# A selective scan of four batches and its preparation, put into one stage

## The reference

```python
A = -jnp.exp(A_log)
xp = jnp.einsum('bld,rd->blr', x, x_proj_w)
dt_in, B, C = xp[..., :16], xp[..., 16:32], xp[..., 32:]
dt = jax.nn.softplus(jnp.einsum('blr,dr->bld', dt_in, dt_proj_w) + dt_proj_b)
dA = jnp.exp(dt[..., None] * A)
dBx = dt[..., None] * B[:, :, None, :] * x[..., None]
# over the 512 tokens of a batch:
#   h = dA_t * h + dBx_t ;  y_t = sum over n of h[:, n] * C_t[n]
y = ys + D * x
```

## Time and profile before

| | us |
|---|---|
| runs | 2249.59, 2257.28, 2246.22 (median 2249.59) |
| profiled execution | 2264.58 |
| its span | 2262.8 |
| mean granted clock of TensorE | 0.9 |

### The profile page before, as it was taken

The page is one execution under the profiler, slowest core; times in us unless marked ns, Lnnn a source line. Parts: engine busy times, 40 slices in busy tenths (PEclk is TensorE's granted clock), DMA queues, the critical chain, the costliest instruction groups (busy, mean ns, idle before and its releaser), DMA issues. The chain is left out here.

```text
span 2262.8 us, 27810 instructions
## 1 busy us (share of the span) xinstructions
PE 1836.9 (81%) x8232; PEld 1117.8 (49%) x8232; DVE 1625.3 (72%) x2905; ACT 808.6 (36%) x1301; POOL 734.1 (32%) x582
## 2 busy tenths in 40 slices
PE   6287878787759899945994888888864999999998
PEld 2022222222436788833881333333452777787786
DVE  4699999999644466666205888888468777667668
ACT  5243434333211344421222777777523111111112
POOL 2676767665250466665002000000021333113100
PEclk7599999999878689866996999999985999999999
DMA  8111111110130688854544333333000000000002
GB/s 302 23 42 38 37 38 35 39 33 15 35 135 14 205 278 285 287 180 130 195 194 126 87 95 91 91 94 87 4 30 28 29 29 29 1 29 29 1 1 75
DMA packets 102032, 197.64 MB, mean 87 GB/s; under 512 B 17257, under 2 KB 34025, under 8 KB 101019
## 3 DMA queue, kind: packets, MB, share of 16 engines
q1 hardware_dynamic: 96795, 179.46, 24.7%
q0 software_dynamic: 5120, 16.78, 2.3%
HBM read 130.72 MB, written 63.05 MB: 86 GB/s over the span
## 5 line engine op out<-in xcount | busy, mean ns | idle before, releaser
L1527 DVE TENSOR_REDUCE att_top<-att_first 128x1 f32<-128x512 f32 x512 | 332.4, 686 | 104.0 <-PE att_first L1407 96.2
L421 PE MATMUL scan_y<-scan_hc,all_ident 128*128 128x512 f32 x512 | 294.8, 663 | 102.2 <-DVE scan_hc L381 102.2
L355 POOL TENSOR_TENSOR scan_dbx<-ssm_U,scan_bbc 128x512 f32<-128x512 f32 x256 | 316.0, 1267 | 135.6 <-DVE scan_h L390 101.9
L390 DVE TENSOR_TENSOR_SCAN scan_h<-scan_da,scan_dbx 128x512 f32<-128x512 f32 x256 | 310.4, 1213 | 23.6 <-POOL scan_dbx L355 20.0
L1489 ACT ACTIVATE att_prob<-att_second 128x1024 f32<-128x1024 f32 x256 | 248.0, 1022 | 88.5 <-PE att_second L1427 83.1
L366 ACT ACTIVATE scan_da<-ssm_DT,ssm_A 128x512 f32 x256 | 176.7, 691 | 271.5 <-DVE scan_h L390 271.4
L421 PEld LDWEIGHTS scan_y<-scan_hc,all_ident 128*128 128x128 f32 x512 | 79.0, 194 | 314.7 <-DVE scan_hc L381 314.0
L1673 POOL TENSOR_TENSOR pairs_raw<-pairs_raw,pairs_scales 128x512 f32<-128x512 f32 x42 | 42.4, 1044 | 526.6 <-DMA pairs_raw<-in_w 526.6
L1803 ACT ACTIVATE ffn_silu<-ffn_pg 128x256 f32<-128x256 f32 x112 | 43.1, 385 | 414.7 <-PE ffn_pg L130 414.7
L1407 PE MATMUL att_first<-att_ks,att_qs 48*128 48x512 f32 x512 | 133.9, 512 | 63.3 <-DVE att_top L1527 48.5
L128 PE MATMUL ffn_pg<-pairs_wh,last_XH 128*128 128x512 f32 x448 | 180.3, 402 | 1.7 <-PEq L431 1.7
(11 more groups left out here) (272 smaller groups left out, 3917.4 us busy)
## 6 DMA issues: line engine op xcount, KB each, us to landing
mlps_raw<-in_w SPq DMA_DIRECT2D x26, 769.0 KB, 6.0
exp_raw<-in_w SPq DMA_DIRECT2D x24, 769.0 KB, 6.0
scan_bbc<-brow_dram SPq DMA_DIRECT2D x64, 256.0 KB, 3.1
sorted_x<-pre_zero SPq DMA_DIRECT2D x4, 3072.0 KB, 15.4
exp_x<-sorted_x SPq DMA_DIRECT2D x48, 256.0 KB, 3.9
sorted_y<-exp_y SPq DMA_DIRECT2D x48, 256.0 KB, 3.8
att_qs<-qk_dram SPq DMA_DIRECT2D x192, 64.0 KB, 2.2
att_ks<-qk_dram SPq DMA_DIRECT2D x192, 64.0 KB, 2.2
```

The source lines that it names most:

```text
L355: nc.gpsimd.tensor_tensor(dbx[:, i % (2 * KC), :], g.U[:, c, bass.ts(b, NB)], bbc[:, n % RING, :], ALU.mult).then_inc(dbx_ready, 1)
L390: nc.vector.tensor_tensor_scan(h[:, i % HRING, :], da[:, i % 2, :], dbx[:, i % (2 * KC), :], 0.0, ALU.mult, ALU.add).then_inc(h_ready, 1)
L421: mm = pe.matmul(y[:, c, :], g.ident[:], hc[:, i % 2, :], start=(m == 0), stop=(m == STATE - 1))
L1527: nc.vector.tensor_reduce(top[w % 2][:, qt, item:item + 1], p_first[first_place(m) % FIRSTS][:], AX.X, ALU.max).then_inc(max_done, 1)
```

## The change

The two stages become one, `ssm`. Only batch 0 is prepared ahead of the first scan, by short instructions of one block each; batch b + 1 is prepared while batch b is scanned, and the magnitudes and positive parts of batch b + 2 are read then as well.

- Lists are unrolled over 64 states (4 batches x 16). Buffers of dt, u, mag, pos hold two batches.
- One ACT copy takes all 80 rows. B's and C's rows are both stored to HBM.
- C is split by VectorE into two float32r parts (`split_c`), at partitions 64 and 96, and spread by one product over both (`spread`), into a `cbc` of one bank instead of two. The free bank is `aux`, for rows, z and dt's sums.
- POOL's four products of a state become one of 128x2048, B's row repeated by a stride of zero (`inputs`).
- For c = 3, POOL weighs instead of VectorE (`weigh_last`), with C's row loaded by a broadcast DMA into `cbs`, where `pooled(n)` holds: all but states 5 and 6 of batches 0 to 2.
- For batches 1 to 3 ACT makes the positive part (Relu), 1 + e, its negative rest (Identity) and the mask (Sign); POOL multiplies the logarithm by the mask; PE adds the four parts of dt by products with the identity (`sum_dt`); ACT copies it out.
- The zeros for `sorted_x` go out as 48 DMAs of 256 KB, one per state from n = 4. x of batch 0 is loaded first.
- The sums of batch b - 1 stand between the scans of states 0 and 2 of batch b.

The core of the diff:

```diff
+        def pooled(n):
+            return n // STATE == BATCH - 1 or n % STATE not in (5, 6)
...
+            store_rows(0)
+            for n in range(STEPS):
+                b, m = n // STATE, n % STATE
+                if m == 0:
+                    sp.wait_ge(stored[b % 2], 32 * (b // 2 + 1))
+                if n >= RING:
+                    sp.wait_ge(dbx_ready, n - RING + 1)
+                sp.dma_start(bbc[:, n % RING, :], g.brow_dram[m, b].partition_broadcast(P)).then_inc(b_in[n % RING], 16)
+                if pooled(n):
+                    if by_pool(n) >= RING:
+                        sp.wait_ge(hp_ready, by_pool(n) - RING + 1)
+                    sp.dma_start(cbs[:, by_pool(n) % RING, :], g.crow_dram[m, b].partition_broadcast(P)
+                                 ).then_inc(c_in[by_pool(n) % RING], 16)
...
+            def inputs(n):
+                pool.wait_ge(b_in[n % RING], 16 * (n // RING + 1))
+                if n % STATE == 0:
+                    pool.wait_ge(u_ready, made(n // STATE, LAST))
+                if n >= 2:
+                    pool.wait_ge(h_ready, KC * (n - 1))
+                nc.gpsimd.tensor_tensor(dbx[:, n % 2], u[:, n // STATE % 2],
+                                        bbc[:, n % RING, :].unsqueeze(1).to_broadcast([P, KC, NB]),
+                                        ALU.mult).then_inc(dbx_ready, 1)
...
+                if n >= 2 and pooled(n - 2):
+                    weigh_last(n - 2)
+                if b + 1 < BATCH:
+                    if m in (7, 8):
+                        masked_ln(b + 1, 2 * (m - 7))
+                        masked_ln(b + 1, 2 * (m - 7) + 1)
+                    if m in (11, 12, 13, 15):
+                        scaled_x(b + 1, (11, 12, 13, 15).index(m))
...
+                nc.scalar.activation(da[:, i % 2, :], dt[:, b % 2, c, :], ACT.Exp,
+                                     scale=minus_a[:, c, n % STATE:n % STATE + 1]).then_inc(da_ready, 1)
+                if b + 2 < BATCH:
+                    if j == 8:
+                        copy_rows(b + 2)
+                    if j in (13, 17, 21, 25):
+                        magnitude(b + 2, (j - 13) // 4)
+                    if j in (14, 18, 22, 26):
+                        positive(b + 2, (j - 14) // 4)
                 if b + 1 < BATCH:
+                    if j < 4:
+                        exponential(b + 1, j)
+                    if 4 <= j < 8:
+                        one(b + 1, j - 4)
+                    if 9 <= j < 13:
+                        negative_rest(b + 1, j - 9)
+                    if j == 15:
+                        logarithm(b + 1)
+                    if j in (16, 19, 20, 23):
+                        mask(b + 1, (16, 19, 20, 23).index(j))
+                    if j in (35, 40, 46, 51):
+                        copy_dt(b + 1, (35, 40, 46, 51).index(j))
...
+            split_c(0)
+            for c in range(KC):
+                positive0(c)
+            for c in range(KC):
+                rest0(c)
+                low0(c)
+            for c in range(KC):
+                part0(c)
+            for c in range(KC):
+                masked_ln0(c)
+                sum0(c)
+                scaled_x0(c)
+            split_c(1)
...
+                    if c:
+                        weigh(n, c - 1)
+                    elif n and not pooled(n - 1):
+                        weigh(n - 1, LAST)
...
+                for k, part in enumerate((mag[:, b % 2], u[:, b % 2], pos[:, b % 2], ln)):
+                    mm = pe.matmul(aux[:], g.ident[:], part[:, c, :], start=(k == 0), stop=(k == 3))
...
+                for c in range(LAST):
+                    if c == LAST - 1 and pooled(n) and n + 1 < STEPS:
+                        spread(n + 1)
+                    gather(n, c)
+                    if n >= 2 and c == 0 and pooled(n - 2):
+                        gather(n - 2, LAST)
+                    if b + 2 < BATCH:
                         if m == 0:
+                            project_rows(b + 2, c)
+                        if m == 1 and c == 0:
+                            project_rows(b + 2, LAST)
+                        if 2 <= m < 2 + KC and c == 1:
+                            project_z(b + 2, m - 2)
+                    if b + 1 < BATCH and (m, c) in ((7, 1), (8, 2), (10, 0), (11, 1)):
+                        sum_dt(b + 1, ((7, 1), (8, 2), (10, 0), (11, 1)).index((m, c)))
```

More of the change, by code:

```diff
@@ L238, in _ @@
[L238 to L252 removed]
+                nc.scalar.activation(rows[:, b % 2, :], aux[0:ROWS, :], ACT.Copy).then_inc(rows_copied, 1)
@@ new lines, in z_of, with magnitude @@
+            def z_of(b, c):
+                return y[:, c, :] if b < 2 else aux[:]
+            def magnitude(b, c):
+                act.wait_ge(z_ready, KC * b + c + 1)
+                if b == 2:
+                    act.wait_ge(low0_ready, c + 1)
+                    act.wait_ge(ln_ready, 1)
+                if b > 2:
+                    act.wait_ge(dt_summed, made(b - 2, c))
+                nc.scalar.activation(mag[:, b % 2, c, :], z_of(b, c), ACT.Abs, bias=dtb[:, c:c + 1]).then_inc(mag_ready, 1)
@@ new lines, in project_z @@
+            def project_z(b, c):
+                pe.wait_ge(rows_copied, b + 1)
+                if b == 1:
+                    pe.wait_ge(mag_ready, c + 1)
+                    pe.wait_ge(pos0_ready, c + 1)
+                if b >= 2:
+                    pe.wait_ge(c_lo_ready, b + 1)
+                    pe.wait_ge(pos_ready, KC * (b - 1) + c)
+                out = y[:, c, :] if b < 2 else aux[:]
+                pe.matmul(out, wdt[:, c * P:(c + 1) * P], rows[0:RANK, b % 2, :], start=True, stop=True).then_inc(z_ready, 1)
@@ new lines, in spread, with gather @@
+            def spread(n):
+                b = n // STATE
+                if n % STATE == 0:
+                    pe.wait_ge(c_lo_ready, b + 1)
+                if n:
+                    pe.wait_ge(hc_ready, by_dve(n))
+                pe.matmul(cbc[:], sel[BOTH, n % STATE, :], c_parts[BOTH, b, :], start=True, stop=True).then_inc(c_ready, 1)
+            def gather(n, c):
+                b, m = n // STATE, n % STATE
+                if m == 0:
+                    if b:
+                        pe.wait_ge(y_read, KC * (b - 1) + c + 1)
+                    else:
+                        pe.wait_ge(mag_ready, KC + c + 1)
+                        pe.wait_ge(pos_ready, made(1, c))
+                if c == LAST and pooled(n):
+                    k = by_pool(n)
+                    pe.wait_ge(hp_ready, k + 1)
+                    pe.matmul(y[:, c, :], g.ident[:], hp[:, k % 2, :], start=(m == 0),
+                              stop=(m == STATE - 1)).then_inc(y_pool, 1)
+                else:
+                    k = by_dve(n) + c
+                    pe.wait_ge(hc_ready, k + 1)
+                    pe.matmul(y[:, c, :], g.ident[:], hc[:, k % 2, :], start=(m == 0),
+                              stop=(m == STATE - 1)).then_inc(y_own, 1)
```

498 lines of the change are left out of this document (290 added, 208 removed).

## The result

The kernel after takes 2182.23 us (median of 4 runs, 2181.62 to 2184.00) against 2249.48 (4 runs, 2246.22 to 2257.28): a ratio of 0.9697 [0.9672, 0.9723], 67 us less. Forecast were 2163 in a range of 2140 to 2200. The profiled execution took 2182.81 us for a span of 2181.1, where the sum made against the profiled execution of before gave 2178.1.

A forecast was written before the change was run, and what follows sets the result against it. The scan was taken to run at VectorE's pace. Gains of 66.2 us at the start and 20.3 in the scan sum to 86.5, taken from the median 2249.59 to give 2163 us, range 2140 to 2200.

The forecast's parts named there:

- in the scan (20.3): Scan stage: 437.1 us against 457.4, with VectorE's work, stalls and the end counted; gain 20.3 us.
- First scan: Start: three of four preparations leave the front, first scan at 39.0 instead of 105.2 us; gain 66.2 us.
- The rival to which I gave 0.20: Start: POOL's three products between VectorE's triples exclude them, costing 3.8 us, total 2167; chance 0.20.
- Sums of dt: Scan, PE: the next spread and gather wait behind dt's products, 0.8 us late at nine places; 7.2 us.
- Logarithm: Scan, ACT: logarithm with two table loads delays the next decay, stalling VectorE 2.0 us in three batches; 6 us.
- POOL: nothing: Scan, POOL: falls behind in rounds 11 to 13 and 15 beyond its slack, 1.5 us a batch; 4.5 us.
- The rival that POOL becomes the bound: Scan: wide product or longer queue takes 5.6 us, rounds slow to 7.5, total 2197; chance 0.18.
- the low clock: Whole stage: PE stays at 1.2 GHz, a round needs 7.4 us, total 2312, slower; chance 0.03.
- End: End of the scan: the last weighing is POOL's, 1.27 for 0.58 and a hand-over; 1 us.
- VectorE's work: Scan: 256 steps less 58 weighings, plus batch sums and splits of C; 418.4 us.
- SP: Scan, SP: loads of B and C and one clear per round, B's ring four deep; cost nothing.
- Sign loads no table: Scan, ACT: the rival was that Sign needs its own table, 12 us over 12 masks, total 2175; chance 0.12.

The follow-up runs named there:

- the run with the later wait: Kernel after, with POOL's first product waiting for all four u parts instead of one: 2180.32 us, 0.9651 of the kernel before.
- the run with one product: Kernel after, with one product instead of four in each sum of dt for batches 1 to 3: 2154.59 us, 0.9610 of the kernel before.
- the repeat: The kernel after, run again without edit: 2165.56 us, 0.9639 of the kernel before.
- the one without table loads: Kernel after, with an exponential in place of the logarithm in batches 1 to 3: 2166.06 us, 0.9588 of the kernel before.

## Why the prediction was right, and where its terms were off

The direction, the mechanism and the range held. The gain of the stage was 78, forecast 86.5: 62.4 at the start (66.2) and 16.1 in the scan (20.3). That the scan came so close is in part luck. A stall of 4.5 us that never came made up for nearly all of the 4.6 that the sums of dt cost beyond their term. The forecast of 2163 was 19 us low, 8 in the stage and 11 behind it.

- **First scan at 42.8, not 39.0.** Up to ACT's logarithm the chain ran as worked out: copy at 15.75 (16.3), first magnitude 17.55 (18.1), table load 23.52 (23.7), logarithm ending at 26.72 (26.9). Then L489 took 1.64 instead of 0.69, three times: 2.9 of the 3.8 us. The other 0.9 are short instructions that each take a little more than a quarter of the wide one (a mask, a sum and a product 2.05 for 1.92, rest and low 1.06 for 1.02, the split 1.44 for 1.3). The rival to which I gave 0.20, that the two engines exclude each other at the start, was right, with 2.9 instead of its 3.8. The row that spoke for it (rest at 5.55) I had discounted as another form; the right weight was the larger one. The Trainium skill, "SBUF — State Buffer", section "Who interferes with whom", names this pair, and the trace agrees: 1.64 beside POOL's product, 0.69 without (the run with the later wait), and 0.67 for weighings with an input in PSUM.
- **Sums of dt: 11.75, not 7.2.** The place and the cause held, as the run with one product shows. I worked out a delay of 0.8 from the starts of records; measured were 1.18 at the three places and 0.37 at (8, 2), where I had none. The term that was too small is the chain gather, sum, spread, weighing: the weighing began 103.70 - 98.62 = 5.1 us behind the start of the gather, where I had the spread done at 4.8.
- **Logarithm: 6.1, forecast 6.** The 5.2 us from start to start and the second decay's 0.69 are the 5.9 of my sum.
- **POOL: nothing, forecast 4.5.** POOL has 47.9 us of idle time ahead of its products, 46.4 of it for the scans. A round of VectorE was 6.25 as forecast; the term was wrong in POOL's own, 5.7 us instead of 5.9 and 6.92 with a product for u instead of 7.15. Three of these in a row put it 3 x 0.67 = 2.0 us behind, and the inputs, two states deep, cover that. Nor does it need VectorE to be late at the sums: with one product in a sum it isn't, and POOL still costs nothing. The rival that POOL becomes the bound fell with it: 4524 ns for the wide product, under the 4.7 that I had named as its limit, and 1279 for a weighing.
- **Idles ahead of other weighings: 2.3 us, not in the sum.** 1.73 of them stand at the scan's beginning, with TensorE's granted clock at 0.50 (1.2 GHz) just before. In the repeat the same place cost 0.46 and others more, 3.1 in all. That the clock is their cause was not tested: they lie behind stretches at a low clock (0.66 from 75, 0.80 from 190), but other such stretches cost nothing. As a rival for the whole stage the low clock fell: 0.94 and 0.95.
- **End 0.96, forecast 1. VectorE's work 420.2, forecast 418.4**, by what is left of 441.3 behind the idle time. The 1.8 are not work: 19 idles at 0.11 us beyond their bracket make about 2.
- **SP: nothing, as forecast.** POOL's waits in the stage are put down to VectorE's scans and u and to TensorE, none to a DMA.
- **Sign loads no table.** Behind the first one of all (L326) the loads are the 8 around the four logarithms, 4 at L395 and 4 at L422; none stands ahead of a mask. By the Trainium skill, "ScalarE: Activation LUTs", section "Table sets: the hidden batching unit", relu, copy, identity and abs are in every set, and the trace agrees; sign, which it doesn't list with them, needed no load behind an exponential either.

So the stage is 3.8 us short at the start and 4.2 in the scan (4.6 at the sums, 2.3 ahead of other weighings, 1.8 by the idles' tails, less 4.5 for POOL; the logarithm and the end add nothing). The 11 us between the stage's 78 and the 67 of the first runs are not in the two stages: the repeat gave 78.1, and the stage of the experts, 367.9 and 356.1 us in the two profiles of the kernel after, differs by as much without an edit. Why that stage varies was not tried; a lower clock goes with a longer stretch over the thirteen profiles, and which is the cause stays open. Not tried by themselves are the one wide product for four, the one copy for three and the 48 small clears; for them there are only the traces, in which none of them stands in VectorE's way.

## What to carry to other kernels

Where work is moved into a stage that one engine sets, count for each moved piece what is queued behind it on its own engine until the leading engine wants the next thing, and move producer and consumer together: a sum put later without its copy only moved the wait from one queue to the other. Look at each pair of operations that will newly overlap on VectorE and POOL: for the scan, one operand in PSUM decided between no cost and the length of the other's instruction. One SBUF input is no safe sign either: `rest` has only one and took 5.55 us beside POOL's product, 1.23 without. And measure a change of one stage by that stage's end in the trace, with a repeat of the same kernel beside it, before asking where a few microseconds of the total went.

## What the runs showed of the hardware that was not expected

- The exclusion holds for the scan too, and both sides pay: 7.38 us for two scans and 2.20 for POOL's weighing, against 2.34 and 1.28. In a loop in which each needs the other, both stand: VectorE's scans are busy or blocked for 616.6 us instead of 305.5, POOL's waits for them grow from 46.4 to 266.3, and a scan of 441 us became one of 738.
- A stage that is equal in two executions of one kernel differed by 12.7 us (372.3 and 359.6), without any edit.
- TensorE's granted clock falls for single stretches of 5 us in the middle of the scan: to 0.66 (150 to 155) and 0.54 (300 to 305) in the kernel after, to 0.51 in the one without table loads. The scan before was at 1.00 in the 95 us of the earlier trace rows. These two stretches of the kernel after cost VectorE nothing; behind the one at 0.51 it waited 1.18 us for a spread.
